# Rotation of queries and keys on GpSimd in the last feed-forward, and an earlier first quarter of the query weights in the second attention

## The reference, cut to what matters

```python
h = _rms(x, w_ln1)
q = (h @ wq + bq).reshape(B, S, N_HEADS, HEAD_DIM)
k = (h @ wk + bk).reshape(B, S, N_KV, HEAD_DIM)
v = (h @ wv + bv).reshape(B, S, N_KV, HEAD_DIM)
def rot(t):
    t1, t2 = (t[..., :D // 2], t[..., D // 2:])
    return jnp.concatenate([-t2, t1], axis=-1)
q, k = (q * cos + rot(q) * sin, k * cos + rot(k) * sin)
scores = jnp.einsum('bqhd,bkhd->bhqk', q, k) * HEAD_DIM ** (-0.5)   # causal
```

```python
def _fp8_linear_pertensor(x, wq, w_scale, in_scale):
    xq = _div_clamp_fp8(x, in_scale)
    return jnp.einsum('bsi,oi->bso', xq * in_scale, wq) * w_scale
ln_out = _ln(hidden_states, ln_w, ln_b)
q = _ln(_fp8_linear_pertensor(ln_out, wq, wq_scale, q_in_scale), qln_w, qln_b)   # heads of 128
k = _ln(_fp8_linear_pertensor(ln_out, wk, wk_scale, k_in_scale), kln_w, kln_b)
v = _fp8_linear_pertensor(ln_out, wv, wv_scale, v_in_scale)
```

## Time and profile before

| | before |
|---|---|
| median of 3 executions | 3430.07 us |
| the profiled execution: its own time, its span | 3432.43 us, 3430.4 us |
| busy: PE, DVE, ACT, POOL | 83%, 66%, 43%, 9% |
| mean granted clock of PE | 0.917 |
| start of the second attention to its first scores | 511.8 to 560.3 us |
| projection, rotation and stacks of the last feed-forward | 3043.9 to 3117.5 us |

### The profile page before, as it was taken

One profiled execution on the slowest core, in us unless ns is written; L12 is line 12 of the kernel. 1 busy time (PEld: TensorE's weight loads), 2 busy tenths in 40 slices (PEclk: granted clock), 3 DMA queues, 4 the chain that ended last, 5 costly groups with the idle time before them and its releaser, 6 DMA issues. The chain is left out here.

```text
span 3430.4 us, 46419 instructions
## 1 busy us (share of the span) xinstructions
PE 2853.3 (83%) x15010; PEld 1845.2 (54%) x15010; DVE 2262.3 (66%) x5492; ACT 1480.6 (43%) x3134; POOL 310.7 (9%) x339
## 2 busy tenths in 40 slices
PE   7886995777789999945999999935679999857898
PEld 4334664666667777723777777724323232234576
DVE  5674337877777787756444444477999999767432
ACT  4452224666655556543222222212356666724322
POOL 0000003111221111000000000031110000001100
PEclk9898996999999999966999999967789999977899
DMA  1002003000000000003000000001000000020000
GB/s 56 1 2 83 1 1 123 13 1 7 13 7 7 7 1 1 1 32 123 1 1 1 0 0 0 0 19 38 7 1 1 1 1 1 1 93 2 1 1 12
DMA packets 37904, 56.91 MB, mean 17 GB/s; under 512 B 6400, under 2 KB 25792, under 8 KB 36416
## 3 DMA queue, kind: packets, MB, share of 16 engines
q1 hardware_dynamic: 37696, 54.35, 4.7%
HBM read 52.99 MB, written 1.05 MB: 16 GB/s over the span
## 5 line engine op out<-in xcount | busy, mean ns | idle before, releaser
L2665 ACT ACTIVATE a_exps<-psum,a_ln 128x512 f32<-128x512 f32 x512 | 314.6, 684 | 191.5 <-PE psum L2595 191.5
L2736 DVE TENSOR_REDUCE a_half_max<-psum 128x1 f32<-128x1024 f32 x256 | 311.3, 1219 | 13.1 <-PE psum L2578 6.5
L843 DVE SCALAR_TENSOR_TENSOR f_silu<-f_silu,psum 128x352 f32<-128x352 f32 (+2 forms) x88 | 50.4, 572 | 245.3 <-ACT f_silu L818 245.3
L1516 PE MATMUL psum<-a_probs_t,a_vals 128*128 128x256 f32 x768 | 193.9, 389 | 17.0 <-ACT a_probs_t L1656 17.0
L2595 PE MATMUL psum<-a_qs,a_ks 99*128 99x512 bf16 x512 | 173.5, 388 | 34.8 <-ACT a_exps L2665 22.9
L1496 PE MATMUL psum<-a_k_t,a_q_t 128*128 128x256 f32 (+1 forms) x512 | 194.7, 505 | 3.0 <-DVE a_k_t L1805 2.6
L1638 ACT ACTIVATE a_normed<-psum,a_head_bias,a_head_scale 128x128 f32<-128x128 f32 x448 | 168.5, 462 | 62.6 <-DVE a_head_bias L1790 62.6
L1018 DVE TENSOR_REDUCE a_neg_max<-psum 128x2 f32<-128x1024 f32 x64 | 78.4, 1225 | 177.2 <-PE psum L1013 177.2
L1664 ACT ACTIVATE a_probs<-psum,a_neg_max 128x256 f32<-128x256 f32 (+1 forms) x256 | 147.0, 583 | 94.8 <-DVE a_neg_max L1810 94.6
L2780 DVE TENSOR_SCALAR a_probs<-a_exps 128x1024 bf16<-128x1024 f32 x256 | 175.0, 684 | 14.1 <-ACT a_exps L2665 13.9
L1810 DVE TENSOR_REDUCE a_neg_max<-psum 128x2 f32<-128x512 f32 (+1 forms) x128 | 122.2, 954 | 93.3 <-PE psum L1496 93.0
(11 more groups left out here) (475 smaller groups left out, 6168.0 us busy)
## 6 DMA issues: line engine op xcount, KB each, us to landing
a_w_raw<-in_L_xattn_wproj_dram SPq DMA_DIRECT2D x8, 512.0 KB, 3.8
f_w_silu<-in_L_ffn_gate_dram SPq DMA_DIRECT2D x1, 2112.0 KB, 10.5
f_w_mul<-in_L_ffn_up_dram SPq DMA_DIRECT2D x1, 2112.0 KB, 15.1
a_probs<-in_ctx_t_dram SPq DMA_DIRECT2D x4, 512.0 KB, 5.0
f_w_silu<-in_L_ffn_Wu_dram SPq DMA_DIRECT2D x1, 2048.0 KB, 7.8
...
```

The source lines that it names most:

```text
L1516: mm = pe.matmul(core.bank(OUT)[:, 0:S], vals[:, quad % 2, j, (h // 2) * P:(h // 2 + 1) * P], probs_t[:, g % 2, j, :], start=(j == 0), sto ...
L2665: act.activation(exps[:, n % UNITS, :], core.bank(LOGITS + u), ACT.Exp, bias=ln255[:, :]).then_inc(exp_ready, 1)
L2736: v.tensor_reduce(half_max[:, h, t, half:half + 1], ring(("scores", s)), AX.X, ALU.max, negate=True).then_inc(ring_free, 1)
```

## The change

In the last feed-forward VectorE's loop is cut in two functions. `project(t)` adds the biases and writes queries and keys to one of two buffers `raw_qk`; `stack_parts_of(t)` scales and splits one of two buffers `rot_qk`. VectorE runs project(t), then stack_parts_of(t-1). Between them GpSimd rotates tile t with the same six operations. PE turns the stacks of tile t-2 after the projection of tile t.

In the second attention SP loads the first quarter of the query weights as the second DMA, right after `cols`, which has a semaphore of its own. ScalarE scales this quarter before it copies the turned tiles, not after. VectorE quantizes once before slot -6 and leaves the other two to the ends of slots -6 and -5.

```diff
--- before.py
+++ after.py
...
@@ -1402,7 +1402,8 @@
         with nc.Block() as block:
             @block.sync
             def _(sp):
-                sp.dma_start(cols[:, :], dram["L1_cols"]).then_inc(small_in, 16)
+                sp.dma_start(cols[:, :], dram["L1_cols"]).then_inc(cols_in, 16)
+                sp.dma_start(q_raw[:, 0, :, :], feature_rows(dram["L1_xattn_wq"])[:, :, q_columns(0)]).then_inc(q_in0, 16)
                 for i, name in enumerate(("wq_scale", "wk_scale", "wv_scale", "wqx_scale")):
                     sp.dma_start(scales[:, i:i + 1], dram["L1_xattn_" + name].partition_broadcast(P)).then_inc(small_in, 16)
                 for i, name in enumerate(("proj_in_scale", "proj_w_scale")):
@@ -1420,7 +1421,6 @@
                         sp.wait_ge(parts_step, 2 * (j - 1))
                     sp.dma_start(w_raw[:, j % 2, :, :], proj_rows[:, j * HPQ:(j + 1) * HPQ, :]).then_inc(PROJ_IN[j % 2], 16)
 
-                load_q(0)
                 for name, c in (("wk", KV0), ("wv", V0)):
                     sp.dma_start(w_all[:, 0, :, c:c + G * P], feature_rows(dram["L1_xattn_" + name])).then_inc(w_in0, 16)
                 load_q(1)
@@ -1603,14 +1603,8 @@
 
             @block.scalar
             def _(act):
-                act.wait_ge(small_in, 7 * 16)
-                for t in range(NT):
-                    act.wait_ge(token_full, t + 1)
-                    for k in range(DK):
-                        last = act.activation(ln_t[:, k, t * P:(t + 1) * P], core.bank(4 + t % 4)[:, k * P:(k + 1) * P], ACT.Identity,
-                                              bias=cols[:, LNB + k:LNB + k + 1], scale=cols[:, LNW + k:LNW + k + 1])
-                    last.then_inc(token_ready, 1)
-                act.wait_ge(coefs_ready, 1)
+                act.wait_ge(small_in, 6 * 16)
+                act.wait_ge(cols_in, 16)
 
                 def scale_q(p, n):
 
@@ -1622,6 +1616,15 @@
                         act.mul(q_w[:, 0, k, q_columns(n)], w, cols[:, s:s + 1])
                         last = act.mul(w, w, cols[:, s:s + 1])
                     last.then_inc(q_scaled, 1)
+
+                scale_q(0, 0)
+                for t in range(NT):
+                    act.wait_ge(token_full, t + 1)
+                    for k in range(DK):
+                        last = act.activation(ln_t[:, k, t * P:(t + 1) * P], core.bank(4 + t % 4)[:, k * P:(k + 1) * P], ACT.Identity,
+                                              bias=cols[:, LNB + k:LNB + k + 1], scale=cols[:, LNW + k:LNW + k + 1])
+                    last.then_inc(token_ready, 1)
+                act.wait_ge(coefs_ready, 1)
 
                 def keep_out(g):
                     p, col = g // H // B, R_SMOOTH + g // H // B * H + g % H
@@ -1672,7 +1675,7 @@
                     last.then_inc(probs_ready, 1)
 
                 for g in range(FIRST, LAST):
-                    if g in q_split_at:
+                    if g in q_split_at and g > FIRST:
                         scale_q(*q_split_at[g])
                     if 0 <= g - 2 < HEADS:
                         keep_out(g - 2)
@@ -1713,7 +1716,8 @@
                     v.bn_aggr(moments[:, t, :], stats[:, t, :])
                 v.drain()
                 v.tensor_scalar(shifted[:, :], moments[:, :, 1], EPS, None, ALU.add).then_inc(var_ready, 1)
-                v.wait_ge(small_in, 7 * 16)
+                v.wait_ge(small_in, 6 * 16)
+                v.wait_ge(cols_in, 16)
                 v.reciprocal(recips[:, :], cols[:, INS:INS + 40])
                 v.tensor_tensor(scales2[:, 0:4], scales[:, 0:4], scales[:, 0:4], ALU.mult)
                 v.tensor_scalar(cols[:, AFF:AFF + 2], cols[:, AFF:AFF + 2], P ** -0.5, None, ALU.mult)
@@ -1835,8 +1839,7 @@
                     v.scalar_tensor_tensor(x, core.bank(SUM).rearrange("p (t d) -> p t d", t=TB), out_scale[:, 0:1], x,
                                            ALU.mult, ALU.add).then_inc(sum_free, 1)
 
-                for i in range(3):
-                    quantize(0, i)
+                quantize(0, 0)
                 for g in range(FIRST, LAST):
                     if g >= H + 2 and (g - 2) % H == 0:
                         add((g - 2) // H - 1)
@@ -1854,6 +1857,8 @@
                         turned(unit_at[g - 2])
                     if g in unit_at:
                         coefs(unit_at[g])
+                    if g in (FIRST, FIRST + 1):
+                        quantize(0, g - FIRST + 1)
                     batch, i = g // H + 1, g % H - QUANT_SLOT
                     if g >= 0 and (batch, i) in xq_no:
                         quantize(batch, i)
@@ -2827,7 +2832,7 @@
         mean_sq = sb("mean_sq", [P, NT])
 
         work = sb("work", [P, 6, 2 * D])
-        qk, turned = work[:, 0:2, :], work[:, 2:4, :]
+        raw_qk, turned, rot_qk = work[:, 0:2, :], work[:, 2:4, :], work[:, 4:6, :]
         SLOTS = 2 * B
         probs = work[:, :, :].rearrange("p a n -> p (a n)").rearrange("p (r n) -> p r n", r=SLOTS)
         above, same = (work[:, i, :].rearrange("p (t e j) -> p t e j", t=NT, e=E) for i in range(2))
...
@@ -2927,6 +2933,23 @@
                                 base=0, pattern=[[1, E], [-1, E]], channel_multiplier=0).then_inc(consts_ready, 1)
                 g.wait_ge(consts_ready, 6)
 
+                halves = lambda a: a.rearrange("p (h two d) -> p h two d", two=2, d=HALF)
+                g.wait_ge(small_in, SMALL * 16)
+                for t in range(NT):
+                    src, dst = halves(raw_qk[:, t % 2, :]), halves(rot_qk[:, t % 2, :])
+                    cos = rotary[:, 0, t % TB, :].unsqueeze(1).broadcast_to([P, 2 * H, HALF])
+                    sin = rotary[:, 1, t % TB, :].unsqueeze(1).broadcast_to([P, 2 * H, HALF])
+                    m_cos, m_sin = halves(turned[:, 0, :]), halves(turned[:, 1, :])
+                    g.wait_ge(raw_ready, t + 1)
+                    for part in range(2):
+                        g.tensor_tensor(m_cos[:, :, part, :], src[:, :, part, :], cos, ALU.mult).then_inc(rotate_step, 1)
+                        g.tensor_tensor(m_sin[:, :, part, :], src[:, :, 1 - part, :], sin, ALU.mult).then_inc(rotate_step, 1)
+                    g.wait_ge(rotate_step, 4 * (t + 1))
+                    at_least(g, stack_ready, 2 * (t - 1))
+                    g.tensor_tensor(dst[:, :, 0, :], m_cos[:, :, 0, :], m_sin[:, :, 0, :], ALU.subtract).then_inc(rot_ready, 1)
+                    g.tensor_tensor(dst[:, :, 1, :], m_cos[:, :, 1, :], m_sin[:, :, 1, :], ALU.add).then_inc(rot_ready, 1)
+                    g.wait_ge(rot_ready, 2 * (t + 1))
+
                 for i in range(STEPS):
                     diagonal = probs[:, i % SLOTS, :].rearrange("p (k n) -> p k n", n=P)[:, 0:3:2, :]
                     g.wait_ge(probs_ready, i + 1)
@@ -2968,9 +2991,11 @@
                             mm = pe.matmul(core.bank(2 * (t % 2) + c)[:, 0:w], xn_t[:, k, t * P:(t + 1) * P], w_qkv[:, k, a:a + w],
                                            start=(k == 0), stop=(k == DK - 1))
                     mm.then_inc(proj_full, 1)
-                    if t >= 1:
-                        turn(2 * t - 2)
-                        turn(2 * t - 1)
+                    if t >= 2:
+                        turn(2 * t - 4)
+                        turn(2 * t - 3)
+                for i in range(2 * NT - 4, 2 * NT - 2):
+                    turn(i)
                 turn(2 * NT - 2)
                 turn(2 * NT - 1)
                 pe.wait_ge(stack_free, 4 * NT)
@@ -3120,35 +3145,32 @@
                 v.drain()
                 rms(2)
                 v.wait_ge(small_in, SMALL * 16)
-                halves = lambda a: a.rearrange("p (h two d) -> p h two d", two=2, d=HALF)
-                for t in range(NT):
+                def project(t):
                     r = t % 2
                     v.wait_ge(proj_full, t + 1)
                     v.tensor_tensor(vals[:, :, t, 0:DH], core.bank(2 * r + 1)[:, 0:D].rearrange("p (h d) -> p h d", h=H),
                                     bias[:, 2 * D:].rearrange("p (h d) -> p h d", h=H), ALU.add)
-                    v.tensor_tensor(qk[:, 0, :], core.bank(2 * r), bias[:, 0:2 * D], ALU.add).then_inc(proj_free, 1)
-                    v.drain()
-
-                    src = halves(qk[:, 0, :])
-                    cos = rotary[:, 0, t % TB, :].unsqueeze(1).broadcast_to([P, 2 * H, HALF])
-                    sin = rotary[:, 1, t % TB, :].unsqueeze(1).broadcast_to([P, 2 * H, HALF])
-                    m_cos, m_sin = halves(turned[:, 0, :]), halves(turned[:, 1, :])
-                    for part in range(2):
-                        v.tensor_tensor(m_cos[:, :, part, :], src[:, :, part, :], cos, ALU.mult)
-                        v.tensor_tensor(m_sin[:, :, part, :], src[:, :, 1 - part, :], sin, ALU.mult)
-                    v.drain()
-                    dst = halves(qk[:, 1, :])
-                    v.tensor_tensor(dst[:, :, 0, :], m_cos[:, :, 0, :], m_sin[:, :, 0, :], ALU.subtract)
```

(19 more changed lines are left out.)

3 lines of the change are left out of this document (2 added, 1 removed).

## The result

The changed kernel takes 3437.68 us (median of 9 runs, 3432.97 to 3439.42) against 3429.93 for the kernel before in the same comparison (9 runs): ratio 1.0026, 95% interval 1.0015 to 1.0036. I had forecast 3426.4 and a range up to 3436. The profiled execution took 3434.52 us, span 3432.8.

The account below looks back on a forecast made before the run. VectorE was taken to set the pace in the last feed-forward and at the second attention's start. Gains of 3.5 and 0.2 us sum to 3.7: from 3430.07 to 3426.4 us, forecast's own range 3422 to 3430, overall range 3416 to 3436.

Parts of the forecast that it names:

- L1726 "like the reduction: 0": Second attention: VectorE's eight normalizing operations, 2.67 us, lose nothing beside GpSimd's low part; up to 2.3 us if blocked.
- rival D: Second attention: L1726 is blocked by GpSimd, the rest as forecast; 3428.7 us, chance 0.10.
- Stall of the coefficient, 2.3: Second attention: VectorE's coefficient (L1788) stands behind GpSimd's low part of the second quarter, 2.5 us; stall 2.3 us.
- Idle until the first statistics, 2.1: Second attention: after the first quantization VectorE waits 2.1 us for PE's unit, an idle not there before.
- From there the streams are the same: Second attention: from the unit of keys, begun at 550.3 instead of 550.51, everything runs as before; gain 0.2 us.
- Term of the second attention: Second attention's share of the forecast: gain 0.2 us; 2.3 more if the stall misses, 2.3 less if L1726 is blocked.
- Turns with GpSimd in the last feed-forward: VectorE and GpSimd alternate, delaying VectorE 1.78 us a tile; tile 7.59 instead of 8.15 us, gain 3.5 us.
- The 0.14 us outside the exclusion: VectorE and GpSimd meeting: about 0.14 us of each operation passes while it waits for the other engine.
- The letter of the Trainium skill's rule: Last feed-forward: shared ports locked for the whole instruction; tile 9.1 us, total 3437; chance 0.17 together with B.
- A: Last feed-forward: meeting GpSimd costs VectorE nothing; tile 5.81 us, end 16 us earlier, 3414 us; chance 0.13.
- B: Last feed-forward: GpSimd keeps its place over four products; end 6.2 us later, 3436; chance 0.17 with the rule's letter.
- C: Last feed-forward as forecast, but the second attention's coefficient slips in before the low part; 3424 us, chance 0.10.

Follow-up runs that it names:

- the part alone: Kernel before with only the second attention's part of the change, last feed-forward as before: 3436.57 us, ratio 1.0019; again 3435.67 us, ratio 1.0017.
- pure delay: Kernel before plus 14 statistics of a tile on VectorE ahead of the second attention's first quantization: 3429.34 us, ratio 0.9998; again 3429.89 us, 1.0003.
- tiny operations: Kernel before with the last feed-forward's change, GpSimd's six operations cut to a few numbers, stacks reading the unrotated tile: 3412.48 us, ratio 0.9952.

## Why the prediction was wrong, step by step

- **L1726 "like the reduction: 0".** This step failed. What rival D assumed came true, though not its time of 3428.7: 2.12 us were lost (4.79 - 2.67). I had read the 0.33 us between its starts as an unhurried pace, and that spacing does not show the pace: by the durations above a normalization moves 1.9 numbers a ns, and the reduction that I likened it to 0.96 (0.69 us for 512, 1.22 for 1024 in the profile before). The Trainium skill, page "SBUF — State Buffer", section "Who interferes with whom", says that a VectorE instruction with at most one SBUF input, outside the 2-port modes, does not contend, and names `tensor_scalar` among those that can enter these modes and then contend. The traces agree with both, if the doubled pace is taken as the sign of such a mode: normalizations were held in two places (2.67 to 4.79 and to 4.69), statistics were not (2.71 beside 2.35 us of GpSimd).
- **Stall of the coefficient, 2.3:** right, 2.31 in place of 0.23.
- **Idle until the first statistics, 2.1:** 2.93. PE did not start when the quantization ended (530.47) but at 531.29, when ScalarE had made its last copy; I had left that wait out.
- **"From there the streams are the same":** failed. By the marks the unit of keys is 2.3 to 2.9 us late instead of 0.2 early (D's 2.1 and the longer idle), and the next quarter 4.0 on average (49.3 in five traces against 45.3 in seven). The order of work is the same from there, but PE's pace is not: the value products behind the keys take 2.9 to 3.6 us in place of 1.9 or 3.0. I had priced VectorE's gaps and put nothing for PE. That the gap of 7 us is what sends PE to its lower level is not shown: the same level stands after pauses of 1.7 and 2.1 us too.
- **Term of the second attention:** forecast -0.2, measured +6.4 and +7.0 for the part alone. The marks account for some 4, the stage's length for 5.5 (987.7 - 982.2). The rest, and why a pure delay of 4.8 us costs nothing, stay open. So that the stalls cause the loss is shown only in part. With the quantizations spread and one meeting the mean is 3432.4 and 3432.7 instead of 3436.3. With none it is still 3432.1, 2.8 above the kernel before, though its keys' mark is 1.1 earlier than there. And a late start as such is not what is paid for.
- **Turns with GpSimd in the last feed-forward:** the mechanism was right, in order and number (six of ten stretched), and nothing else eats the gain (tiny operations: -18 us). The size was wrong: product 0.72 instead of 0.61, delay 8.19 - 5.81 = 2.38 a tile instead of 1.78. Seven tiles of 0.6 are 4.2 us; -3.5 became about +1 in the trace (65.8 against 65.0) and +0.6 in the time. I had this case in the text (3.5 more if a product costs 0.72) and took the third feed-forward's row as near enough. It has the same size, short rows and repeated cosines too; what it lacks of the price isn't shown. The 0.14 us outside the exclusion held: the cast begun at 3064.59 ends 0.28 us after GpSimd's product (3065.38 against 3065.10), of 0.43 alone. The letter of the Trainium skill's rule, a tile of 9.1 us, was too long.
- **Rivals A, B, C:** A and B out (tile neither 5.8 nor over 9), C out (the coefficient did not slip in).
- **Sum:** 4 us from the last feed-forward and some 7 from the second attention make the 11 by which I missed.
